# A decoder layer on one core: the attention's steps in another order on four engines, written out batch by batch

## Chip, core and metric

One core of one Trainium2 chip. The metric is the device time of one execution in microseconds (us). TensorE is called PE in the profile, VectorE DVE, ScalarE ACT, GpSimd POOL, and SyncE's DMA queue SPq.

## What is computed

One decoder layer on 16 batches of 128 rows of 128 numbers (float32): self-attention with 16 heads of 8 columns and rotary positions, a correlation step against a context, and a feed-forward part with 8 experts of which each row takes 2. After each of the three the input is added and the rows are normalised. Cut to the part that the change touches:

```python
qkv = jnp.einsum('bsd,ed->bse', x, w_qkv)            # x: (16, 128, 128)
q, k, v = ...                                         # 16 heads of 8
q, k = _apply_rope(q, cos, sin), _apply_rope(k, cos, sin)
scores = jnp.einsum('bhsd,bhtd->bhst', q, k) * SCALE
attn = jax.nn.softmax(scores, axis=-1)
out = jnp.einsum('bhst,bhtd->bhsd', attn, v)
x = _layernorm(x + out @ w_out.T + b_out)             # then correlation, then experts
```

## The kernel before

Each engine has a program of its own, a list of steps written by hand. Steps wait on semaphores for what they read and for buffers to come free; an engine never starts a step before the one ahead of it in its list. So the lists alone set the order, and no scheduler does.

**The stages.** The attention goes over the batches n = 0 to 15, several in flight at once. Then come the correlation step (one spectrum over all batches) and the experts in four groups of four batches. Only the attention's lists and the few steps beside them are touched here.

**One batch of the attention**, with the step's name in the code and the line of its instruction:

- PE `qkv(n)` (L965, L966) projects the batch; ACT `keep_qkv` (L706) copies the result from PSUM.
- The rotation is `rope_products` (L432, L438) and `rope_sum` (L444), on DVE for n = 0 and 1, on POOL from then on. Queries and keys are cut into three bf16 pieces, so that bf16 matmuls keep float32's precision: ACT `first_piece` (L719), POOL or DVE `remainder` (L450), ACT `second_piece` (L723) and `second_copy` (L727), POOL or DVE `third_piece` (L456). All land in `stack`, of which there are two.
- The keys are turned by PE `k_transposes` (L1003) and copied by ACT `kT_copy` (L732). The queries of batches 0 to 2 are turned by PE and copied by DVE; from batch 3 on SPq does it with a transposing DMA, `q_transpose` (L341).
- PE `scores(n, u)` (L981), u = 0 and 1 for the two halves of the heads, is reduced to row maxima by DVE `maxima` (L1383). `pieces_of_maxima` (L463, L465) makes two bf16 rows of them, PE `maxima_transpose` (L1028) turns these, ACT `mT_copy` (L745) copies them, and SPq `spread_maxima` (L348, two DMAs) spreads them into the query tile.
- PE `scoresT(n, u)` (L997) makes the same scores transposed, less the maxima; ACT `softmax_exp` (L737) takes the exponential into `early`; PE `weighted(n, u)` (L1042 and L1046) makes the weighted sums of `v_pad` and the denominators. `v_pad` is filled by POOL `pad_v` (L506).
- DVE `reciprocal` (L1394) and `divide` (L1399); PE `project` (L1059); DVE `residual_sum` (L1406), `statistics_of_rows` (L1419), `mean_and_variance` (L1424); POOL `inverse_deviation` (L493, L496); DVE `normal_rows` (L469).

`score_pair` and `scoreT_pair` each hold one half at a time: `scores(n, 1)` waits until `maxima(n, 0)` has read, and `scoresT(n, 1)` until `softmax_exp(n, 0)` has.

In the middle a loop `for k in range(8, 16)` gives every engine the same list for each k, with batch k at its first step and batch k-6 at its last ones. Ahead of it stands a list that fills the pipeline, behind it one that empties it.

**Beside the attention.** Four `w1_high_piece(i)` on ACT (L702) and four `w1_low_piece(i)` on POOL (L521) cut the experts' weight `w1` into two parts; piece i on POOL waits for piece i on ACT, and PE wants all four before its first expert matmul. `expand_v(g)` on POOL (L529) lays out the correlation's values. `residual(g)` on DVE (L1413) adds a bias to four batches of the input. `keep_clock(n)` on PE (L945, L951) is n matmuls into a free place, whose result nobody reads.

**Behind the attention**, untouched: ACT copies a spectrum (L751 to L753), makes two small parts (L842, L844) and takes the square root of the last batch's variance (`sd`, L846); DVE ends the last rows (L1549, L1552), PE ends the spectrum, DVE multiplies (L1561, L1565, L1566) and makes `lag` in two instructions (L1568, L1571), for which PE's next matmul (L1228) waits. POOL adds a bias to four groups of rows (`add_cross_bias`, L601): the first as soon as the last row is normal, the other three only when DVE has made `wsel` (L1588).

The two instructions that make `lag` read two operands from SBUF, as do L432 to L456, L465 and L1413:

```python
dve.scalar_tensor_tensor(lag[:, 0, :], sinm, reim[:, 1:2], part[:, 0, :], ALU.mult, ALU.add)
dve.scalar_tensor_tensor(lag[:, 1, :], sinm, reim[:, 0:1], part[:, 1, :], ALU.mult, ALU.subtract)
```

## Time and profile before

| | us |
|---|---|
| median of 3 runs | 232.91 |
| lowest and highest run | 232.44 and 234.08 |
| profiled execution, first to last instruction | 229.2 |
| PE busy | 215.3 (94%) |
| DVE busy | 181.3 (79%) |
| ACT busy | 142.5 (62%) |
| POOL busy | 111.6 (49%) |

The profile gives the profiled execution as its span, 229.2 us, which is 3.7 us under the median of the runs; those lie ahead of the first and behind the last instruction. The busy shares are averages over stages: in the attention all four engines are busy, in the experts PE and DVE alone. The end of a matmul is modelled, so that a PE that is never idle in a row may still have small gaps, which show between the starts.

### The profile page before, as it was taken

How to read it: one execution, taken by the hardware profiler on the slowest of the kernel's cores; microseconds unless marked ns; L12 is line 12 of the kernel's file. 1: busy time of each engine (PE TensorE's matmuls, PEld its weight loads, DVE VectorE, ACT ScalarE, POOL GpSimd, SP SyncE). 2: the span in 40 equal slices, each digit the busy share in tenths (PEclk: the TensorE clock that was granted, in tenths of full speed). 3: DMA queues.
4: the chain of work that ended last, by engine and by line, in shares of the span. 5: the costliest groups of instructions: out<-in, count | busy, mean ns of one | idle time of the engine just before them, and what ended most of it. 6: DMA issues, size and time to landing. Idle time of an engine off the chain costs nothing.

```text
span 229.2 us, 7210 instructions
## 1 busy us (share of the span) xinstructions
PE 215.3 (94%) x2724; PEld 184.4 (80%) x2724; DVE 181.3 (79%) x622; ACT 142.5 (62%) x248; POOL 111.6 (49%) x219
## 2 busy tenths in 40 slices
PE   8989899999999989999999999999999999999970
PEld 7766677778777667778887999789988999889970
DVE  0589998999899899776755779897798868875885
ACT  2488899999999995674489300991029610596112
POOL 5089889999889995513630400252002600040484
PEclk9999999999999999999999999999999999999996
DMA  5951534765569941000000000001000100001001
GB/s 149 286 124 34 106 61 51 171 133 119 138 125 156 156 90 19 14 3 1 3 0 0 3 0 1 0 3 46 4 0 0 46 3 1 0 4 46 1 16 34
DMA packets 32455, 12.32 MB, mean 54 GB/s; under 512 B 19907, under 2 KB 32291, under 8 KB 32419
## 3 DMA queue, kind: packets, MB, share of 16 engines
q1 hardware_dynamic: 31554, 11.48, 24.5%
q8 instruction: 22, 0.36, 0.7%
q10 hardware_dynamic: 864, 0.36, 0.6%
q14 instruction: 15, 0.11, 0.2%
HBM read 6.33 MB, written 1.05 MB: 32 GB/s over the span
## 4 chain that ended last, share of the span: by engine, by line
PE 81%; DVE 6%; DMA 5%; ACT 3%; issue 2%; SPq 1%; DVEq 0%; ACTq 0%
PE bank L1326 13%; PE scoreT_pair L1326 12%; PE score_pair L1298 11%; PE scoreT_pair L1298 8%; PE bank L1042 6%; PE bank L1046 5%; DMA qT_all<-mT 5%; PE bank L965 4%; PE scoreT_pair L997 4%; PE bank L1003 3%; PE score_pair L981 3%; PE scoreT_pair L945 2%; PE bank L1059 2%; ACT early L737 2%; PE bank L940 1%
## 5 line engine op out<-in xcount | busy, mean ns | idle before, releaser
L1383 DVE TENSOR_REDUCE rowmax<-score_pair 128x8 f32<-128x1024 f32 x32 | 39.0, 1218 | 3.3 <-PE score_pair L981 2.0
L608 POOL TENSOR_TENSOR ve<-mv,table 128x4 f32<-128x4 f32 (+1 forms) x12 | 3.3, 277 | 78.1 <-DVE mv L1743 60.2
L737 ACT ACTIVATE early<-scoreT_pair 128x1024 f32<-128x1024 f32 x32 | 32.9, 1027 | 6.0 <-PE scoreT_pair L997 5.9
L1326 PE MATMUL bank<-w,early 128*128 128x128 f32 x256 | 30.1, 276 | 0.0
L1326 PE MATMUL scoreT_pair<-w,early 128*128 128x128 f32 x256 | 29.9, 275 | 0.0
L1326 PEld LDWEIGHTS bank<-w,early 128*128 128x128 f32 x256 | 29.5, 192 | 0.3
L1326 PEld LDWEIGHTS scoreT_pair<-w,early 128*128 128x128 f32 x256 | 29.2, 192 | 0.0
L1298 PE MATMUL score_pair<-x2T_part,w_part 128*128 128x512 f32 x108 | 28.4, 397 | 0.0
L880 ACT ACTIVATE early<-score_pair,b 128x512 f32<-128x512 f32 x38 | 26.0, 691 | 3.2 <-PE score_pair L1298 2.6
L1042 PE MATMUL bank<-early,v_pad 128*32 128x128 f32 x512 | 26.5, 279 | 0.4 <-DVE attnT L1399 0.3
L1046 PE MATMUL bank<-early,head_ones 128*32 128x128 f32 x512 | 25.8, 273 | 0.0
L1298 PEld LDWEIGHTS score_pair<-x2T_part,w_part 128*128 128x128 f32 x108 | 19.6, 188 | 4.9 <-ACT early L880 1.4
L1298 PE MATMUL scoreT_pair<-x2T_part,w_part 128*128 128x512 f32 x78 | 19.9, 391 | 0.0
L1394 DVE RECIPROCAL rden<-bank 128x128 f32<-128x128 f32 x16 | 15.3, 956 | 4.2 <-PE bank L1046 4.1
L880 ACT ACTIVATE early<-scoreT_pair,b 128x512 f32<-128x512 f32 x26 | 17.6, 690 | 0.0
L1298 PEld LDWEIGHTS scoreT_pair<-x2T_part,w_part 128*128 128x128 f32 x78 | 14.6, 188 | 3.0
L732 ACT ACTIVATE kT_all<-bank 128x1024 bf16<-128x1024 bf16 x16 | 16.3, 1020 | 0.2 <-PE bank L1003 0.2
L1042 PEld LDWEIGHTS bank<-early,v_pad 128*32 128x32 f32 x512 | 12.7, 109 | 4.5 <-ACT early L737 1.4
L1046 PEld LDWEIGHTS bank<-early,head_ones 128*32 128x32 f32 x512 | 15.4, 110 | 0.0
L1731 DVE SCALAR_TENSOR_TENSOR x_ext<-bank,gate,x_ext 128x128 f32<-128x128 f32 x32 | 11.1, 346 | 4.7 <-PE bank L1326 4.7
L997 PE MATMUL scoreT_pair<-qT_all,kT_all 64*128 64x128 bf16 x256 | 12.7, 218 | 1.8 <-ACT early L737 0.7
L1731 DVE SCALAR_TENSOR_TENSOR x_ext<-scoreT_pair,gate,x_ext 128x128 f32<-128x128 f32 x32 | 11.1, 346 | 4.0 <-PE scoreT_pair L1326 3.7
(229 smaller groups left out, 474.0 us busy)
## 6 DMA issues: line engine op xcount, KB each, us to landing
w<-in_w SPq DMA_DIRECT2D x8, 256.0 KB, 3.8
x_ext<-in_x SPq DMA_DIRECT2D x4, 256.0 KB, 5.4
qT_all<-mT SPq DMA_DIRECT2D x32, 32.0 KB, 2.3
early<-in_xT SPq DMA_DIRECT2D x3, 256.0 KB, 4.5
early<-in_ctxT SPq DMA_DIRECT2D x3, 256.0 KB, 5.1
out<-qkv_all SPq DMA_DIRECT2D x3, 256.0 KB, 2.3
table<-in_tables SPq DMA_DIRECT2D x1, 321.0 KB
qT_all<-stack SPq DMA_TRANSPOSE x13, 3.4
```

The source lines that it names most:

```text
L732: act.activation(kT[n % DEEP][:, :, :], turned_slots, ACT.Copy).then_inc(s["k_T"], 1)
L737: act.activation(prob[n % 2][:, 2 * u:2 * u + 2, :, :], scoreT_pair[:, :].rearrange("p (i j s) -> p i j s", i=2, j=QUAD), ACT.Exp, scale=S ...
L880: act.activation(hT[:, c, :], hidden_bank(g, c)[:, :], ACT.Relu, bias=b1[:, c:c + 1])\
L965: pe.matmul(qkv_bank[:, 0:3 * D + XC], xT[:, n, :], wqkv[:, :], start=True, stop=True)
L997: mm = pe.matmul(scoreT_pair[:, (QUAD * side + j) * S:(QUAD * side + j + 1) * S], kT[n % DEEP][rows, 2 * j + u, :], qT[n % DEEP][rows, 2 * ...
L1042: pe.matmul(sum_bank(n)[WIDE * j:WIDE * (j + 1), 0:S], v_pad[n % 2][:, j, i, :], prob[n % 2][:, i, j, :], start=(i == 0), stop=(i == QUAD ...
L1046: mm = pe.matmul(sum_bank(n)[WIDE * j:WIDE * (j + 1), S:2 * S], head_ones[:, i * WIDE:(i + 1) * WIDE], prob[n % 2][:, i, j, :], start=Fals ...
L1298: mm = pe.matmul(hidden_bank(g, c)[:, :], w1_part[:, w, c * P:(c + 1) * P], x2T_part[:, x, :], start=(k == 0), stop=(k == 2))
L1326: mm = pe.matmul(expert_bank[k % 4][:, e4 * D:(e4 + 1) * D], hT[:, f, n * P:(n + 1) * P], w2[:, f, :], start=(c == 0), stop=(c == CH - 1))
L1383: dve.tensor_reduce(rowmax[:, H // 2 * u:H // 2 * (u + 1)], score_pair[:, :].rearrange("p (r t) -> p r t", t=S), AX_X, ALU.max).then_inc(s ...
L1394: dve.reciprocal(rden[:, :], sum_bank(n)[:, S:2 * S]).then_inc(s["rden_ready"], 1)
L1731: dve.scalar_tensor_tensor(total, product, weight, total, ALU.mult, ALU.add).then_inc(s["summed"], 1)
```

## The change

Only calls are moved. The loop over k on each of the four engines is replaced by its 8 rounds written out, each with an order of its own, and some steps ahead of and behind it move too. The steps themselves, their waits, their buffers and SPq's list are as before. Cut to what the text speaks of:

```diff
 # GpSimd, from batch 15's pieces on
-            pad_v(12)
-            w1_low_piece(0)
-            w1_low_piece(1)
-            w1_low_piece(2)
-            pad_v(13)
-            w1_low_piece(3)
-            pad_v(14)
-            inverse_deviation(8)
+            pad_v(12)
+            inverse_deviation(7)
+            w1_low_piece(0)
+            inverse_deviation(8)
+            pad_v(13)
...
+            inverse_deviation(12)
+            expand_v(1)
+            w1_low_piece(1)
             inverse_deviation(13)
             inverse_deviation(14)
+            w1_low_piece(2)
+            expand_v(2)
+            expand_v(3)
+            w1_low_piece(3)
 # ScalarE
             softmax_exp(11, 1)
-            w1_high_piece(0)
-            w1_high_piece(1)
-            w1_high_piece(2)
-            w1_high_piece(3)
             mT_copy(13)
             softmax_exp(12, 0)
             kT_copy(15)
             softmax_exp(12, 1)
+            w1_high_piece(0)
...
             softmax_exp(15, 1)
+            w1_high_piece(1)
+            w1_high_piece(2)
+            w1_high_piece(3)
 # TensorE, the fill
             qkv(0)
             keep_clock(3)
+            keep_clock(3)
             qkv(1)
-            keep_clock(3)
             turn_projection()
...
+            scores(2, 0)
             scoresT(0, 0)
-            scores(2, 0)
...
+            scores(3, 0)
             k_transposes(4)
             maxima_transpose(2)
             scoresT(1, 0)
-            scores(3, 0)
             qkv(7)
 # TensorE, the middle: round k = 9 of the eight
-                scoresT(k - 6, 0)
-                scores(k - 4, 0)
-                qkv(k)
-                project(k - 7)
-                scoresT(k - 6, 1)
-                scores(k - 4, 1)
-                weighted(k - 6, 0)
-                weighted(k - 6, 1)
-                k_transposes(k - 2)
-                maxima_transpose(k - 4)
+            scores(5, 0)
+            scoresT(3, 0)
+            maxima_transpose(4)
+            qkv(9)
+            k_transposes(6)
+            project(2)
+            scoresT(3, 1)
+            scores(5, 1)
+            weighted(3, 0)
+            weighted(3, 1)
 # VectorE, the fill
             third_piece(dve, 0)
-            residual(0)
             remainder(dve, 1)
             qT_copy(0)
-            keep_turned()
+            residual(0)
```

On TensorE, at the start of round k = 9 (`bank4` takes `qkv`, `bank5` the turned keys, `bank7` the turned maxima and the projection). Before, from the last two steps of round 8 on:

```order
L1003 MATMUL bank5<-ident16,stack0 128x128 x8
L1028 MATMUL bank7<-ident16,mstack 128x128
L997 MATMUL scoreT_pair<-qT_all,kT_all 128x128 x8
L981 MATMUL score_pair<-kT_all,qT_all 128x128 x8
L965 MATMUL bank4<-wqkv,early 128x392
L966 MATMUL bank4<-xwq,early 128x8
L1059 MATMUL bank7<-wo,attnT 128x136
L997 MATMUL scoreT_pair<-qT_all,kT_all 128x128 x8
```

The changed kernel at the same place (its lines stand 104 higher: L1085 is `scores`, L1101 `scoresT`, L1107 the keys' transposes, L1132 the maxima's):

```order
L1085 MATMUL score_pair<-kT_all,qT_all 128x128 x8
L1101 MATMUL scoreT_pair<-qT_all,kT_all 128x128 x8
L1132 MATMUL bank7<-ident16,mstack 128x128
L1069 MATMUL bank4<-wqkv,early 128x392
L1070 MATMUL bank4<-xwq,early 128x8
L1107 MATMUL bank5<-ident16,stack0 128x128 x8
L1163 MATMUL bank7<-wo,attnT 128x136
L1101 MATMUL scoreT_pair<-qT_all,kT_all 128x128 x8
```

The same eight pieces of work stand between the last `weighted` and the second `scoresT`: `scores` has gone to the front, the transposes behind it.

On ScalarE, from batch 15's keys on. Before (L702 is `w1_high_piece`):

```order
L732 ACTIVATE kT_all<-bank 128x1024
L737 ACTIVATE early<-scoreT_pair 128x1024
L702 ACTIVATE w_part<-w 128x512 x4
L745 ACTIVATE mT<-bank 128x128
L737 ACTIVATE early<-scoreT_pair 128x1024
L732 ACTIVATE kT_all<-bank 128x1024
```

The changed kernel, from its last `kT_copy` (L780) on (L785 is `softmax_exp`, L750 `w1_high_piece`, L793 `mT_copy`, L807 loads a function table):

```order
L780 ACTIVATE kT_all<-bank 128x1024
L785 ACTIVATE early<-scoreT_pair 128x1024
L750 ACTIVATE w_part<-w 128x512
L793 ACTIVATE mT<-bank 128x128
L785 ACTIVATE early<-scoreT_pair 128x1024 x2
L793 ACTIVATE mT<-bank 128x128
L785 ACTIVATE early<-scoreT_pair 128x1024 x4
L750 ACTIVATE w_part<-w 128x512 x3
L807 ACT_TABLE_LOAD
```

One of the four cuts of `w1` has moved back by four steps, the other three to behind the last exponential.

On GpSimd, around the end of the attention. Before:

```order
L493 TENSOR_TENSOR ve<-mv,table 128x1
L496 TENSOR_TENSOR rs<-ve,table 128x1
L601 TENSOR_TENSOR x_all<-x_all,bias 128x4x128
L635 TENSOR_TENSOR gate_w_part<-gate_w,gate_w_part 128x8
L601 TENSOR_TENSOR x_all<-x_all,bias 128x4x128 x3
```

The changed kernel (L649 is `add_cross_bias`):

```order
L529 COPY early<-x_ext 128x512
L521 TENSOR_TENSOR w_part<-w,w_part 128x512
L493 TENSOR_TENSOR ve<-mv,table 128x1
L496 TENSOR_TENSOR rs<-ve,table 128x1
L493 TENSOR_TENSOR ve<-mv,table 128x1
L496 TENSOR_TENSOR rs<-ve,table 128x1
L521 TENSOR_TENSOR w_part<-w,w_part 128x512
L529 COPY early<-x_ext 128x512 x2
L521 TENSOR_TENSOR w_part<-w,w_part 128x512
L649 TENSOR_TENSOR x_all<-x_all,bias 128x4x128
L683 TENSOR_TENSOR gate_w_part<-gate_w,gate_w_part 128x8
```

Three cuts of `w1` and three layouts of the values now stand around and behind the last two `inverse_deviation`, ahead of the first bias addition.

## Rows read from the trace of the kernel before

**Rows 1.** Busy time by stretch: us, then each engine's, PE's clock, DMA share, GB/s

```profile
0.00:33.20 33.20, 29.75 (x388) 23.82 (x390) 23.19 (x49) 22.63 (x40) 22.19 (x49) 1.00 0.53 124
33.20:73.20 40.00, 40.00 (x889) 31.44 (x888) 36.61 (x80) 38.14 (x65) 36.52 (x81) 1.00 0.63 130
73.20:98.90 25.70, 23.83 (x582) 17.86 (x580) 22.41 (x50) 21.02 (x31) 18.36 (x37) 1.00 0.49 69
98.90:107.90 9.00, 8.26 (x72) 7.51 (x69) 6.98 (x31) 4.51 (x14) 2.17 (x4) 1.00 0.00 1
```

**Rows 2.** Timeline of PE and its loads, one round: start, us, engine, line, what

```profile
55.06 0.40 PE L997 MATMUL scoreT_pair<-qT_all,kT_all 64*128 64x128 bf16 x8
...
56.57 0.43 PE L1042 MATMUL bank<-early,v_pad 128*32 128x128 f32 x8
...
57.59 0.62 PE L1003 MATMUL bank<-ident,stack 128*128 128x128 bf16 x8
```

**Rows 3.** Waits from 33 to 73 us: total, times, longest

```profile
ACT early L737 <- PE scoreT_pair L997: 1.9, 8, 0.2
...
PEld bank L1042 <- ACT early L737: 0.9, 6, 0.2
```

**Rows 4.** Timeline of SPq, then DMA issues at 44.2 and 59.2: KB, us to landing

```profile
58.75 1.24 SPq L348 DMA_DIRECT2D qT_all<-mT  x2
...
qT_all<-mT SPq DMA_DIRECT2D x2, 32.0 KB, 3.0
...
qT_all<-mT SPq DMA_DIRECT2D x2, 32.0 KB, 2.6
```

**Rows 5.** Timeline of the fill, ACT, DVE and PE

```profile
11.84 0.83 ACT L719 ACTIVATE stack<-qk 128x768 bf16<-128x768 f32 x1
...
12.34 0.88 DVE L1413 TENSOR_TENSOR x_ext<-x_ext,bias 128x512 f32<-128x512 f32 x1
...
22.72 0.40 PE L997 MATMUL scoreT_pair<-qT_all,kT_all 64*128 64x128 bf16 x8 [0.32 <-DMA qT_all<-mT]
...
28.40 0.39 PE L981 MATMUL score_pair<-kT_all,qT_all 48*128 48x128 bf16 x8
...
30.03 0.40 PE L997 MATMUL scoreT_pair<-qT_all,kT_all 64*128 64x128 bf16 x8
```

**Rows 6.** Timeline of ACT, batches 12 and 13

```profile
81.48 2.20 ACT L702 ACTIVATE w_part<-w 128x512 fp32r<-128x512 f32 x4
83.56 0.29 ACT L745 ACTIVATE mT<-bank 128x128 bf16<-128x128 bf16 x1
```

**Rows 7.** Timeline behind the last exponential, ACT, DVE and POOL

```profile
102.01 0.30 ACT L846 ACTIVATE sd<-mv,table 128x1 f32<-128x1 f32 x1 [0.78 <-DVE mv L1424]
...
100.72 0.18 DVE L1424 BATCH_NORM_AGGREGATE mv<-st 128x2 f32<-128x6 f32 x1
...
104.69 0.34 DVE L1568 SCALAR_TENSOR_TENSOR lag<-table,reim,part 65x128 f32<-65x128 f32 x1
...
100.98 0.19 POOL L493 TENSOR_TENSOR ve<-mv,table 128x1 f32<-128x1 f32 x1 [3.62 <-DVE mv L1424]
101.25 0.55 POOL L496 TENSOR_TENSOR rs<-ve,table 128x1 f32<-128x1 f32 x1
```

**Rows 8.** Timeline of POOL and DVE where both read SBUF, and where one does

```profile
78.59 1.73 POOL L529 COPY early<-x_ext 128x512 f32<-128x512 f32 x3
...
82.21 3.73 POOL L521 TENSOR_TENSOR w_part<-w,w_part 128x512 fp32r<-128x512 f32 x3 [0.47 <-ACT w_part L702]
...
81.55 0.23 DVE L463 CAST mstack<-rowmax 128x16 bf16<-128x16 f32 x1
...
85.39 0.59 DVE L463 CAST mstack<-rowmax 128x16 bf16<-128x16 f32 x1
...
9.90 0.42 DVE L450 TENSOR_TENSOR rest<-qk,stack 128x256 f32<-128x256 f32 x1
...
13.15 0.61 DVE L450 TENSOR_TENSOR rest<-qk,stack 128x256 f32<-128x256 f32 x1
```

More of the change, by code:

```diff
@@ L1482, in _ @@
             divide(1)
[L1483 to L1493 removed]
+            maxima(4, 0)
+            residual_sum(1)
+            maxima(4, 1)
@@ new lines, in _ @@
+            pieces_of_maxima(dve, 4)
+            reciprocal(2)
+            divide(2)
+            maxima(5, 0)
+            normal_rows(dve, 0)
+            maxima(5, 1)
+            pieces_of_maxima(dve, 5)
+            residual_sum(2)
+            statistics_of_rows(1)
+            reciprocal(3)
+            divide(3)
+            maxima(6, 0)
+            residual_sum(3)
+            statistics_of_rows(2)
+            maxima(6, 1)
+            mean_and_variance(1)
+            pieces_of_maxima(dve, 6)
@@ new lines, in _ @@
+            statistics_of_rows(3)
+            mean_and_variance(2)
+            reciprocal(4)
+            divide(4)
+            maxima(7, 0)
+            maxima(7, 1)
+            normal_rows(dve, 1)
+            residual_sum(4)
+            pieces_of_maxima(dve, 7)
+            reciprocal(5)
+            mean_and_variance(3)
+            statistics_of_rows(4)
+            divide(5)
+            maxima(8, 0)
+            maxima(8, 1)
+            mean_and_variance(4)
+            residual_sum(5)
@@ L1540, in _ @@
             statistics_of_rows(14)
+            normal_rows(dve, 13)
             mean_and_variance(14)
```

360 lines of the change are left out of this document (276 added, 84 removed).

## The prediction

> **What bounds the kernel now.** Read the busy time by stretch first [rows 1]. From 33.2 to 73.2 us the eight rounds of the middle run, 40.0 / 8 = 5.0 us each, and PE has no idle time; ACT is busy 38.1 of the 40, DVE 36.6, POOL 36.5. PE's idle time lies in the fill (33.2 - 29.75 = 3.45, of which about 1.0 is the start) and in the emptying (25.7 - 23.83 = 1.87). Everything behind 107.9 us is as before, so the change is worth what it does to the end of the attention and to the 9 us behind it.
>
> Next one round on PE [rows 2]. I count from T, the start of what follows the second `weighted` (57.59). From T to the second `scoresT` of the next round stand the keys' transposes, the maxima's transpose, `scoresT`, `scores`, `qkv` and `project`: 55.06 - (57.59 - 5.0) = 2.47 us with no gap. From that `scoresT` to the second `weighted` are 1.51 us (56.57 - 55.06), in which PE waits for the exponential: 0.9 us in six rounds [rows 3], 0.15 each. From there to T are 1.02. The three make 5.0. So the loop is closed on PE, but for 0.15 a round in which ACT holds it; ACT in turn waits 0.23 a round for PE [rows 3], and is no bound of its own.
>
> **The change, part by part.**
>
> The middle, 8 rounds. The same matmuls stand between T and the second `scoresT`: 2.47 us again. The exponential still hangs on that `scoresT`, so the 1.51 and the 1.02 stay. What could be won is only the 0.15 where PE waits, and only if work moves from ahead of `scoresT(n, 1)` to behind it; that happens in one round (k = 15, where `project` does). Against it stand a few more changes between float32 and bf16 matmuls, and one round (k = 11) in which DVE gets `normal_rows`, `residual_sum` and `statistics_of_rows` between its maxima and the next `divide`, so that `maxima(8, 0)`, on which `scores(8, 1)` waits, is some 0.2 late. I take 0.0. The ends: 0.9 to the good (every wait of rows 3 gone), and the wait of the rival below to the bad.
>
> The fill. Three things:
> - `residual(0)`, 0.88 us on DVE [rows 5], stood ahead of the second batch's `remainder`. That `remainder`, at 13.15 [rows 8], had its input from 11.84 + 0.83 = 12.67 on [rows 5]; the second `keep_clock(3)` ahead of `qkv(1)` makes that input about 0.2 later, by delaying batch 1, so `remainder` can start near 12.9, 0.25 earlier. `residual(0)` takes some of this back ahead of `third_piece(1)`: I carry 0.15 on, through `scores(0, 0)`, the maxima and the first spread, to `scoresT(0, 0)` at 22.72 [rows 5].
> - `scores(2, 0)` no longer stands behind that DMA wait, which makes DVE's `maxima(2, 0)` some 0.8 earlier. `scoresT(1, 0)` doesn't gain by it: it waits for the next spread, issued from an `mT_copy` that still stands behind `softmax_exp(0, 0)`. So it is again 0.15 earlier.
> - `scores(3, 0)` stood between `scoresT(1, 0)` and `scoresT(1, 1)`: it took the first 0.32 of the 1.63 us from 28.40 to 30.03 [rows 5]. It now stands ahead, in PE's wait.
>
> Together 0.15 + 0.3 = 0.45 us earlier into the middle. Ends: 0 (DVE's chain `reciprocal(0)`, `maxima(3, 0)` takes the end, since two `residual` now stand ahead of it) and 1.0.
>
> The emptying. The four cuts of `w1` on ACT, from 81.48 to 83.56 [rows 6], stood ahead of `mT_copy(13)`. They leave; of their 2.08 us about 0.4 to 0.7 reach the exponentials of batch 12. Later `project(11)` and `project(12)` move ahead of a `scoresT`, or behind, and a spread of maxima (batch 14) is the last to come in both. Following the waits to the last `weighted` I find 0.65 us ahead of before, 0.2 more than at the end of the fill. Ends: 0 and 0.7.
>
> Behind the attention, ACT. Three of the cuts, 3 x 2.08 / 4 = 1.56 us, now stand between the last exponential and `sd`. Before, ACT waited 0.78 for DVE there [rows 7] and 0.52 ahead of the spectrum, 1.30 together. Since the last exponential itself comes about 0.9 earlier and the row that `sd` waits for only 0.65, the new finish of ACT's list falls within 0.1 of that row. Cost 0.05; ends 0 and 0.4.
>
> Behind the attention, POOL. POOL's `inverse_deviation(14)` starts with the batch's variance, 100.98 against DVE's 100.72 [rows 7], and lasts until 101.80. The changed list goes on without a wait: a cut of 1.25 us (3.73 / 3), two layouts of 0.58 (1.73 / 3), a cut of 1.25 [rows 8]. In the times of before that is 101.9 to 103.15, then 104.3, then 105.55; then comes the first bias addition. DVE makes `lag` at 104.69 [rows 7] and right behind it, inside the last cut, and both instructions read two operands from SBUF. In the trace before POOL is idle there. What such an overlap costs is shown in two places [rows 8]. DVE's cast of the maxima takes 0.23 us at 81.55 and 0.59 at 85.39, under the third cut of the row at 82.21, which ends near 85.9; it ends only with it. DVE's `remainder` takes 0.42 us at 9.90 with POOL idle, 0.61 at 13.15 with POOL busy. So DVE waits for the rest of POOL's instruction: 105.55 - 104.69 = 0.86. I take 0.8. Ends: 0 (this form of instruction doesn't wait) and 1.9 (POOL's next 1.25 us instruction gets in between the two).
>
> The Trainium skill says this in "SBUF — State Buffer", section "Who interferes with whom": a VectorE instruction with two SBUF inputs contends with a GpSimd instruction that reads SBUF, and whichever was issued second blocks until the first is done. By that rule, the trace agrees for `remainder` and the cast (0.42 and 0.61 us; 0.23 and 0.59), and no row shows `scalar_tensor_tensor` in that position. With it the sum is the one below; without it, 0.8 less.
>
> The sum: 0.0 - 0.45 - 0.2 + 0.05 + 0.8 = +0.2 us. The span goes from 229.2 to 229.4 and the time from 232.91 to 233.1.
>
> **Rivals.**
> - *`lag` isn't held up.* Then only the lead is left: -0.6, 232.3 us. For it: no row has this form beside POOL, and POOL may be out of step by half a microsecond. Against: POOL is busy without a break for some 4 us around the place.
> - *It is held up twice.* 1.9 in place of 0.8: 234.2 us. For it: POOL's next instruction waits already when the first `lag` ends.
> - *PE's idle time is filled.* The orders differ in every round, and I followed only the waits that bind before. If half of what PE idles in fill and emptying behind the start (2.45 + 1.87) and half the 0.9 of the middle go, that is 2.6 us: 230.3. Against: the fill hangs on two DMA chains that stay.
> - *Slower: the spread of the maxima lands late.* The first `scoresT` of a round comes 0.4 to 0.6 us sooner after T than before, at T or T + 0.23, while its maxima are spread as late as ever: `mT_copy` ends near T + 1.15 (58.75, rows 4), the second DMA is issued 0.62 later and lands 2.6 to 3.0 us after that [rows 4], at T + 4.4 to 4.8, against 5.0. It decides from a landing of 3.3 us on. If the transposed queries, whose `second_copy` in some rounds is later, shift the queue so that landings take 3.6, each round waits 0.3: 8 x 0.3 = 2.4, 235.5 us. Against it: in the rounds seen the landings leave 0.2 to 0.6.
>
> **How the numbers follow.** A change of 1% is about what a measurement of this kernel can tell from none. The forecast (233.1, give or take 0.6) gets 0.38, `lag` free 0.25, held twice 0.13, idle time filled 0.11, late spread 0.13. Under 230.6 lies most of the fourth case, over 235.2 most of the last: faster by over 1% 0.10, within 1% 0.78, slower by over 1% 0.12. The range goes from 231.2 (the ends of fill, emptying and half the middle together) to 235.0, short of the late spread.
>
> **What would show it.** The eight rounds at 5.0 us each with PE never idle. The first `scoresT(1, 0)` near 28.0 and the second `weighted(1, 1)` done near 32.1. No wait of PE for `qT_all` from 33 to 72 us. The last exponential near 96 us and `sd` near 101.4 without a long wait. The first `lag` instruction over 1 us long, with POOL in a cut. The forecast is wrong if a round isn't 5.0 us, by eight times the difference, or if POOL has its last cut behind it before `lag`.

## The result, and the profile after

The changed kernel takes 235.53 us (median of 5 runs, 235.28 to 240.67) where the kernel before takes 232.91 (5 runs, 231.36 to 234.39): ratio 1.015, 95% interval 1.010 to 1.020. A second trial of both gave 236.06 against 231.9, 1.016 (1.013 to 1.019). The forecast was 233.1 and its range ended at 235.0. The 240.67 is of an execution in a second, slower state and doesn't count in the ratio.

The profiled execution took 237.35 us, its span is 235.5 (before 229.2). In every execution whose time and span are both on record the time is 1.75 to 1.95 us over the span. So, as an estimate, the profiled execution of before took some 231.1 us: of the 3.7 us between its span and the median of the runs only half lie ahead of the first and behind the last instruction, and the rest is that this execution was a quick one. The same three stretches as in [rows 1], cut at the same events in the changed kernel:

```profile
35.40:77.40 42.00, 39.56 (x885) 31.26 (x883) 39.48 (x80) 39.20 (x66) 37.24 (x83) 1.00 0.66 118
77.40:102.60 25.20, 23.61 (x578) 18.17 (x580) 20.83 (x50) 19.14 (x28) 12.35 (x30) 1.00 0.49 78
102.60:114.30 11.70, 8.73 (x81) 7.61 (x72) 10.42 (x33) 6.05 (x16) 7.30 (x11) 1.00 0.01 2
```

The fill ends 2.2 us later than before (35.4 against 33.2), the middle takes 42.0 instead of 40.0, the emptying 25.2 instead of 25.7, and what follows 11.7 instead of 9.0. In the middle PE, without idle time before, idles 2.4 us, and DVE is busy 39.5 us with the same 80 instructions that took 36.6.

I set the two traces side by side by events that both have: the first exponential of batches 0, 2 and 10, the last exponential, and the second `x2T_part` of DVE (L1646, L1879 after), from which to the end of the span both need 114.7 us. All are starts.

| us | before | after | difference |
|---|---|---|---|
| start to the first exponential | 23.16 | 25.08 | +1.92 |
| from there to batch 2's | 10.45 | 10.70 | +0.25 |
| batch 2's to batch 10's (the middle) | 40.04 | 42.05 | +2.01 |
| batch 10's to the last exponential | 23.19 | 22.78 | -0.41 |
| from there to the second `x2T_part` | 17.69 | 20.28 | +2.59 |
| from there to the end | 114.67 | 114.66 | 0 |

These are +6.3 us, while the timed runs differ by 2.6 to 4.2. The first line is the reason: it is a matter of the single run, as the next paragraph shows.

**The first line.** The twelve matmuls of the two `keep_clock(3)` in the changed kernel's trace, then in those of three experiments told of below: *tail_undone* and *mt10_early*, which have the changed fill, and *middle_only*, which has the fill of before (its last four are of `keep_clock(2)`). One `keep_clock(3)` shows as six instructions.

```profile
7.03 2.91 PE L1049 MATMUL scoreT_pair<-mean_w 128*128 128x128 f32 x12
```
```profile
5.77 1.58 PE L1049 MATMUL scoreT_pair<-mean_w 128*128 128x128 f32 x12
```
```profile
6.73 1.58 PE L1049 MATMUL scoreT_pair<-mean_w 128*128 128x128 f32 x12
```
```profile
7.03 1.63 PE L1049 MATMUL scoreT_pair<-mean_w 128*128 128x128 f32 x6
...
10.04 1.16 PE L1049 MATMUL scoreT_pair<-mean_w 128*128 128x128 f32 x6
...
11.26 0.61 PE L1049 MATMUL scoreT_pair<-mean_w 128*128 128x128 f32 x4
```

The same instructions in the same list take 0.24 us each in one execution and 0.13 in another. The matmuls of the first 3.7 us have the slow pace in every trace; the step to the faster one comes between 3.8 and 6.7 us in fourteen of the twenty traces and past 8 us in six, in either order of the list. The granted clock reads 1.00 in all of these windows, which is the level of 2.4 GHz, so the record doesn't show it. The 1.9 us are chance. With the step at 3.9 us the changed fill reaches its first exponential at 22.62 and batch 2's at 32.96 (*tail_undone*); with the step near 6 us, as in the trace of before, at 22.94 and 33.62 (*lows_late*), where before needed 23.16 and 33.61. So with the pace of before the changed fill is 0.2 ahead at the first exponential and level at batch 2's. With the step between 4 and 5.1 us in both it is 0.3 to 0.5 ahead at batch 2's (33.20 in *act_regular* and *pool_regular*, 33.54 to 33.72 in *mt10_late*, *end_only* and *keep_ahead*, which have the fill of before).

The fill has a second matter of chance, and only in its changed order. *mt10_early* has the pace of before (its `keep_clock` starts at 6.73 in both), and its first exponential still comes at 24.54. Here are DVE's second `remainder` (L450) and POOL's `rope_products` (L438) in *lows_late* and in *mt10_early*:

```profile
12.56 0.42 DVE L450 TENSOR_TENSOR rest<-qk,stack 128x256 f32<-128x256 f32 x1 [0.54 <-ACT stack L768]
12.57 1.03 POOL L438 TENSOR_TENSOR rot<-qkv_all,table 128x128 f32<-128x128 f32 x2
```
```profile
12.69 0.68 DVE L450 TENSOR_TENSOR rest<-qk,stack 128x256 f32<-128x256 f32 x1 [0.54 <-ACT stack L767]
12.69 0.93 POOL L438 TENSOR_TENSOR rot<-qkv_all,table 128x128 f32<-128x128 f32 x2
```

The two start within 0.01 us of each other, and one holds the other: DVE takes 0.42 and POOL's first 0.68, or DVE 0.68 and POOL's first 0.39. Of the ten traces with the changed fill on all engines seven went the first way and reached the first exponential 10.4 to 10.7 us behind this `remainder`; three went the second (*mt10_early*, *fill_and_round*, *keep_behind*) and needed 11.9, 13.2 and 13.5. With the fill of before it is 10.0 in all nine traces.

**The middle.** DVE's two cuts of the maxima, from 33.6 to 73.6 us before and from 35.8 to 77.8 after (groups by line: count | busy, mean ns | idle ahead):

```profile
L465 DVE TENSOR_TENSOR mstack<-rowmax,mstack 128x16 bf16<-128x16 f32 x8 | 1.6, 196 | 0.3
L463 DVE CAST mstack<-rowmax 128x16 bf16<-128x16 f32 x8 | 1.4, 178 | 0.0
```
```profile
L463 DVE CAST mstack<-rowmax 128x16 bf16<-128x16 f32 x8 | 3.1, 382 | 0.1
L465 DVE TENSOR_TENSOR mstack<-rowmax,mstack 128x16 bf16<-128x16 f32 x8 | 2.6, 328 | 0.3
```

2.7 of the 2.9 us by which DVE's busy time grew are in these sixteen instructions. The timeline of the changed kernel shows how, in the round that became 5.47 us long:

```profile
43.95 0.68 POOL L456 TENSOR_TENSOR stack<-rest,stack 128x256 bf16<-128x256 f32 x1
43.95 0.72 DVE L463 CAST mstack<-rowmax 128x16 bf16<-128x16 f32 x1
...
44.58 0.73 POOL L432 TENSOR_TENSOR rot<-qkv_all,table 128x256 f32<-128x256 f32 x1
44.70 0.66 DVE L465 TENSOR_TENSOR mstack<-rowmax,mstack 128x16 bf16<-128x16 f32 x1
45.27 0.29 DVE L1579 TENSOR_TENSOR y<-bank,x_ext 128x136 f32<-128x136 f32 x1
45.70 0.22 PE L1132 MATMUL bank<-ident,mstack 128*128 128x128 bf16 x1 [0.59 <-DVE y L1579]
45.95 0.28 ACT L793 ACTIVATE mT<-bank 128x128 bf16<-128x128 bf16 x1 [0.59 <-PE bank L1132]
```

Each cut ends with POOL's instruction beside it (44.67 and 44.63, 45.36 and 45.31), and the chain behind it, transpose, copy, spread, is late by that. The transpose itself waits last for `residual_sum` (L1579), which DVE's changed list has behind the cuts of this round and no longer ahead of them: it empties the bank that the transpose writes. Of the sixteen cuts eight are held like this (0.28 to 0.72). In the eight rounds of before the cuts stand beside POOL's `inverse_deviation`, whose two instructions are on 128x1, and none is held:

```profile
57.01 0.19 POOL L493 TENSOR_TENSOR ve<-mv,table 128x1 f32<-128x1 f32 x1
57.06 0.18 DVE L463 CAST mstack<-rowmax 128x16 bf16<-128x16 f32 x1
57.27 0.20 DVE L465 TENSOR_TENSOR mstack<-rowmax,mstack 128x16 bf16<-128x16 f32 x1
57.28 0.59 POOL L496 TENSOR_TENSOR rs<-ve,table 128x1 f32<-128x1 f32 x1
```

The longest round of after is the last, 6.04 us:

```profile
71.79 1.02 ACT L785 ACTIVATE early<-scoreT_pair 128x1024 f32<-128x1024 f32 x1
72.86 0.42 ACT L775 ACTIVATE stack<-rest 128x256 bf16<-128x256 f32 x1
73.18 0.26 ACT L793 ACTIVATE mT<-bank 128x128 bf16<-128x128 bf16 x1
...
73.47 1.27 SPq L348 DMA_DIRECT2D qT_all<-mT  x2
...
77.39 0.40 PE L1101 MATMUL scoreT_pair<-qT_all,kT_all 64*128 64x128 bf16 x8 [0.63 <-DMA qT_all<-mT]
...
77.83 1.02 ACT L785 ACTIVATE early<-scoreT_pair 128x1024 f32<-128x1024 f32 x1 [0.76 <-PE scoreT_pair L1101]
```

`mT_copy(10)` is the only one of the middle that stands behind the batch's exponential and a copy. PE had the transpose ready at 71.80 (71.57 + 0.23); SyncE issues the spread by the copy at 73.18, and 4.2 us later it lets PE go.

**Behind the attention.** DVE, POOL and ACT of the changed kernel, to hold against [rows 7]:

```profile
102.23 1.28 POOL L521 TENSOR_TENSOR w_part<-w,w_part 128x512 fp32r<-128x512 f32 x1 [1.56 <-ACT w_part L750]
102.59 1.00 DVE L469 TENSOR_SCALAR x_all<-y,mv,rs 128x136 f32<-128x136 f32 x1
...
106.22 1.27 POOL L521 TENSOR_TENSOR w_part<-w,w_part 128x512 fp32r<-128x512 f32 x1
106.28 1.28 DVE L469 TENSOR_SCALAR x_all<-y,mv,rs 128x136 f32<-128x136 f32 x1
106.39 0.30 ACT L950 ACTIVATE sd<-mv,table 128x1 f32<-128x1 f32 x1 [0.47 <-DVE mv L1597]
...
107.68 0.99 DVE L1785 TENSOR_SCALAR x_all<-y,mv,rs 128x8 f32<-128x8 f32 x2
...
109.78 1.26 POOL L649 TENSOR_TENSOR x_all<-x_all,bias 128x512 f32<-128x512 f32 x1
109.83 1.30 DVE L1799 TENSOR_SCALAR part<-table,reim 65x128 f32<-65x128 f32 x1
...
111.05 0.34 DVE L1801 SCALAR_TENSOR_TENSOR lag<-table,reim,part 65x128 f32<-65x128 f32 x1
```

`lag` is 0.34 long, as before, and stands beside POOL only for 0.15 us, beside a product on 128x8 (L683, 0.20 long, at 111.01). It is the `tensor_scalar` instructions ahead of it that end with POOL's: `normal_rows` 1.00 and 1.28 instead of 0.34, `part` 1.30 instead of 0.28. What holds `part` is the first bias addition (L649), which the moved pieces have pushed to there; before, it ran at 103.01, ahead of `part`.

### The profile page after: what moved, and what is told of

It reads as the page before. It is cut to its first block, busy times and chain, and to the rows that moved or that the text cites. A ratio compares the mean times of both kernels' runs of the same rounds, so it can differ in the third digit from the quotient of the medians.

```text
span 235.5 us, 7210 instructions
## 1 busy us (share of the span) xinstructions
PE 216.9 (92%) x2724; PEld 186.2 (79%) x2724; DVE 186.6 (79%) x622; ACT 143.9 (61%) x248; POOL 111.4 (47%) x219
## 3 DMA queue, kind: packets, MB, share of 16 engines
q1 hardware_dynamic: 31554, 11.48, 25.2%
## 4 chain that ended last, share of the span: by engine, by line
PE 60%; POOL 11%; DVE 9%; issue 5%; DMA 3%; ACT 2%; SPq 1%; DVEq 0%; POOLq 0%; ACTq 0%
PE bank L1499 12%; PE scoreT_pair L1499 12%; PE score_pair L1471 11%; PE scoreT_pair L1471 8%; PE bank L1146 3%; DMA qT_all<-mT 3%; PE bank L1150 2%; POOL rot L438 2%; PE scoreT_pair L1101 2%; POOL rest L450 2%; POOL qk L444 2%; POOL stack L456 2%; PE score_pair L1085 1%; PE bank L1163 1%; ACT early L785 1%
## 5 line engine op out<-in xcount | busy, mean ns | idle before, releaser
L785 ACT ACTIVATE early<-scoreT_pair 128x1024 f32<-128x1024 f32 x32 | 32.8, 1025 | 5.2 <-PE scoreT_pair L1101 4.5
L780 ACT ACTIVATE kT_all<-bank 128x1024 bf16<-128x1024 bf16 x16 | 16.3, 1018 | 0.3 <-PE bank L1107 0.3
L432 POOL TENSOR_TENSOR rot<-qkv_all,table 128x256 f32<-128x256 f32 x14 | 10.3, 736 | 10.9 <-DVE qk L444 10.2
L1101 PE MATMUL scoreT_pair<-qT_all,kT_all 64*128 64x128 bf16 x256 | 12.7, 218 | 2.6 <-DMA qT_all<-mT 1.3
```

The costliest lines, as they stand in the source:

```text
L432: eng.tensor_tensor(rot[:, 0, :].rearrange("p (h d) -> p h d", d=HD), qkv_all[:, n, 0:2 * D].rearrange("p (h d) -> p h d", d=HD), cosines, ...
L780: act.activation(kT[n % DEEP][:, :, :], turned_slots, ACT.Copy).then_inc(s["k_T"], 1)
L785: act.activation(prob[n % 2][:, 2 * u:2 * u + 2, :, :], scoreT_pair[:, :].rearrange("p (i j s) -> p i j s", i=2, j=QUAD), ACT.Exp, scale=S ...
L1101: mm = pe.matmul(scoreT_pair[:, (QUAD * side + j) * S:(QUAD * side + j + 1) * S], kT[n % DEEP][rows, 2 * j + u, :], qT[n % DEEP][rows, 2 * ...
```

## The experiments

Four questions: what the start costs, what is lost behind the attention, what the middle loses, and whether a gain is left. "Stretch" is from the first exponential of batch 2 to that of batch 10 (before 40.04, after 42.05); "tail" from the last exponential to the last `lag` (before 8.11, after 10.70).

**The changed kernel once more (*again*), no edit.**

> The changed kernel, word for word, a second time. In its first profile the twelve keep_clock matmuls ahead of qkv(1) took 2.69 us (0.224 each), where the kernel before took 0.125 each, and the fill came 1.9 us late; its execution was 1.9 us longer than its other runs. Theory A (the slow first matmuls are chance, and the order costs about 2.6 us elsewhere): the matmuls take about 0.125 each in this profile, the first exponential comes near 23.2 us, and the median stays at 1.010 to 1.020 of before. Theory B (the second keep_clock(3) itself brings the slow matmuls on): 0.22 each again, first exponential near 25.1 us.

1.016 (1.013 to 1.019); the trace again has the slow pace up to past 10 us, stretch 42.4, tail 10.71. That left both theories of the start open; *tail_undone*, with the same list in the fill, decided for chance, and *middle_only* showed the slow pace with the list of before (first exponential 25.02).

**The pieces of the first layer back (*tail_undone*).** In the changed kernel, on ScalarE and GpSimd:

```
 ACT  softmax_exp(11, 1)
+     w1_high_piece(0) ... w1_high_piece(3)
 POOL ...
+     w1_low_piece(0) ... (3), expand_v(1) ... (3)
      inverse_deviation(8) ... inverse_deviation(14)
-     w1_low_piece(2), expand_v(2), expand_v(3), w1_low_piece(3)
```

> The changed kernel with the cuts of w1 and the layouts of the values back where they were: all four w1_high_piece behind softmax_exp(11, 1), the w1_low_piece and expand_v ahead of pad_v(15). Theory A (DVE's chain behind the last exponential is held up by GpSimd's long instructions, 2.5 us of the loss between the last weighted and lag): from the last weighted to lag 6.4 us as before, and the time falls by 2.0 to 2.5 us against the changed kernel, to 0.998 to 1.006 of before. Theory B (that stretch is long because ScalarE's cuts delay the square root): then it should gain 0.5 at most more than GpSimd's moved work alone gives. Rival: the loss sits in the middle and this gives under 1 us.

1.013 (1.008 to 1.017), where theory A had 0.998 to 1.006. The tail is 8.18, and DVE's instructions have their old lengths:

```profile
105.48 0.32 DVE L469 TENSOR_SCALAR x_all<-y,mv,rs 128x136 f32<-128x136 f32 x1
106.13 0.54 DVE L1788 TENSOR_SCALAR x_all<-y,mv,rs 128x8 f32<-128x8 f32 x2
...
108.05 0.28 DVE L1802 TENSOR_SCALAR part<-table,reim 65x128 f32<-65x128 f32 x1
```

So the placement of these pieces makes the whole 2.5 us of the tail. The time fell by less, 1.016 to 1.013 with intervals that overlap: the four cuts in a row ahead of `mT_copy(13)` are back too, and from batch 10's exponential to the last it is 25.2 us instead of 22.8.

**The last pieces later still (*lows_late*).**

```
 POOL inverse_deviation(14)
-     w1_low_piece(2), expand_v(2), expand_v(3), w1_low_piece(3)
      add_cross_bias(0), gate_w_rest()
+     wait for circ_ready; expand_v(2), expand_v(3), w1_low_piece(2), w1_low_piece(3)
```

> The changed kernel, where GpSimd's w1_low_piece(2) and (3) and expand_v(2) and (3) wait for wsel and so run behind lag; ScalarE's cuts stay at the end. If the loss behind the attention is VectorE waiting for GpSimd's instructions, all of them behind inverse_deviation(14) are gone and 1.5 to 2.0 us of the 2.5 come back (the first cut, which holds one normal_rows up, stays). If it is ScalarE's cuts ahead of the square root, nothing comes back.

Half right: the tail is 8.68, 2.0 us back, but the time 1.018 (1.014 to 1.022), nothing gained. Up to the second `x2T_part` it is 20.37 again: the bias additions, pushed back, now hold the normalized rows of the next step (L1877), which take 0.34 each in the changed kernel and here 0.58, 1.30, 1.11 and 0.34:

```profile
114.36 3.70 POOL L645 TENSOR_TENSOR x_all<-x_all,bias 128x512 f32<-128x512 f32 x3
...
115.13 1.80 DVE L1877 TENSOR_SCALAR x<-y,mv,rs 128x128 f32<-128x128 f32 x2
...
117.04 1.37 DVE L1877 TENSOR_SCALAR x<-y,mv,rs 128x128 f32<-128x128 f32 x2
```

**Only the placement of the pieces, in the kernel before (*cuts_late*)**: ScalarE's first cut behind `softmax_exp(12, 1)` and three behind the last exponential, GpSimd's pieces around and behind the last two `inverse_deviation`, all else as before.

> Before, with only the pieces of the first layer and the expansions of v placed as in the changed order: ScalarE's first cut behind softmax_exp(12, 1) and three behind the last exponential, GpSimd's remainders of them and expand_v(1) to (3) around and behind inverse_deviation(13) and (14). Theory A (this placement alone makes the loss behind the attention, by holding VectorE's tensor_scalar operations): last exponential to last lag 10.5 to 10.8 us instead of 8.1; the exponentials of 12 to 15 come up to 0.8 earlier, without four cuts in a row ahead of mT_copy(13); ratio 1.007 to 1.012. Theory B (it needs the changed order of the inverse deviations and VectorE's late rows as well): 8.1 to 9.2 and 0.997 to 1.004.

1.009 (1.006 to 1.013); tail 10.22, two normalizations of 0.9 and two of 0.84 in it:

```profile
104.38 1.77 DVE L469 TENSOR_SCALAR x_all<-y,mv,rs 128x136 f32<-128x136 f32 x2
106.27 1.68 DVE L1788 TENSOR_SCALAR x_all<-y,mv,rs 128x8 f32<-128x8 f32 x2
```

The placement alone makes 2.1 of the 2.6 us. The exponentials of batches 12 to 15 did not come earlier: batch 10's to the last took 23.6.

**The changed order from the last rounds on (*end_only*), and only in the middle (*middle_only*).** Both are the kernel before, with each engine's list switched to the changed one at `weighted(9, 1)`, `mT_copy(11)`, `divide(9)`, `pad_v(11)`, or from `weighted(1, 1)`, `mT_copy(3)`, `divide(1)`, `pad_v(3)` up to there.

> Before up to weighted(9, 1), mT_copy(11), divide(9) and pad_v(11), and from there on the changed order: the last rounds, the emptying, the first layer's pieces and inverse_deviation. Theory A (GpSimd's late pieces stand in DVE's way behind the attention, and that costs 2.6 us whatever stood ahead): last exponential to the last lag 10.6 to 10.8 us against 8.1, the emptying within 0.5 of before, 1.009 to 1.013 of the kernel before. Theory B (they fall there only since the whole middle came 2 us later to the end; handed over on time they are done before the deviations are wanted): last exponential to the last lag 8.1 to 9.0, ratio 0.998 to 1.004.

1.009 (1.006 to 1.013), stretch 40.34, emptying 23.3, tail 10.70: theory A, with the middle handed over on time. One round of the untouched part, around 48 us, took 5.45: PE waits there for a spread of maxima, as it does in *keep_ahead* (5.28) and *mt10_late* (5.75), and not in the trace of before.

> Before, with the changed order on all four engines only in the rounds of the middle: from where weighted(1, 1), mT_copy(3), divide(1) and pad_v(3) end to where weighted(9, 1), mT_copy(11), divide(9) and pad_v(11) do; the fill, the emptying and what stands behind the attention are those of before. Theory A (the rounds of the middle cost about 2.0 us themselves: from the first exponential of batch 2 to that of batch 10 the changed kernel took 42.05 us and before 40.04): 1.0065 to 1.0100 of the kernel before (233.5 to 234.3), the same stretch 41.5 to 42.2 us. Theory B (the middle is late only because the changed fill hands its chains over in another phase, POOL's and the spread's above all): 0.998 to 1.003, the stretch 40.0 to 40.6.

1.019 (1.015 to 1.023). The time is over theory A's 1.010. The stretch is 42.18, as theory A has it; the rest of the loss is where the changed middle meets the old end, with 4.84 us between the two exponentials of batch 10 (2.44 before) and an emptying of 25.99 (23.20). Neither the changed fill nor the changed end is needed for the 2.0 us.

**One copy in the middle, out and in.** *mt10_early* is the changed kernel and *mt10_late* the kernel before, with on ScalarE

```
 mt10_early                      mt10_late
+mT_copy(10)                    -mT_copy(10)
 softmax_exp(9, 0)               softmax_exp(9, 0)
 second_copy(13)                 second_piece(13), second_copy(13)
-mT_copy(10)                    +mT_copy(10)
```

> The changed kernel with one step moved on ScalarE: mT_copy(10) ahead of softmax_exp(9, 0), where every other one of these copies stands, and not behind second_copy(13). Theory A (this place made the round from 71.79 to 77.83 us, 6.04 long: the copy at 73.18, the spread at 73.47, and scoresT(10, 0) at 77.39 waited for it): the round takes 4.9 to 5.1, the kernel 0.9 to 1.1 us less than the changed one (235.0 to 235.2, ratio 1.011 to 1.013). Theory B (DVE and GpSimd hold the end of that round anyway, and PE only waits for whichever is last): the round stays 5.6 to 6.0 and the time within 0.3 us of the changed one's 236.06.

1.012 (1.008 to 1.016), no difference from the changed kernel that the intervals show. The trace:

```profile
71.09 0.28 ACT L793 ACTIVATE mT<-bank 128x128 bf16<-128x128 bf16 x1
71.27 1.02 ACT L785 ACTIVATE early<-scoreT_pair 128x1024 f32<-128x1024 f32 x1
...
71.82 1.26 SPq L348 DMA_DIRECT2D qT_all<-mT  x2
...
76.20 0.40 PE L1101 MATMUL scoreT_pair<-qT_all,kT_all 64*128 64x128 bf16 x8
```

The wait for the spread is gone and the round is 5.37 instead of 6.04, but the exponential ahead of it came 0.2 later, so the stretch is 41.61: 0.45 back, not 1.0, and the emptying took it again (23.3 against 22.8; the changed kernel's second trace has 23.2 as well).

> Before, with one step moved on ScalarE: mT_copy(10) behind softmax_exp(9, 0), second_piece(13) and second_copy(13), as the changed order has it but with no other difference. Theory A (this place costs the round some 1 us, since the spread of these maxima is issued by it and scoresT(10, 0) stands behind the spread's landing): the step from the first exponential of batch 9 to that of batch 10 6.0 to 6.9 us instead of 5.0, the kernel 0.9 to 1.9 us over before (1.004 to 1.008). Theory B (before has slack there that the changed order had lost): 5.0 to 5.4, ratio under 1.002.

1.011 (1.002 to 1.020). The round is 6.16 instead of 5.0 and the emptying 24.15 instead of 23.19. Put into a kernel that had no other fault the step costs its 1.2 us and, in this trace, 0.95 more behind it. The stretch is 41.83: a further 0.75 is the round of 5.75 around 48 us, ahead of the step and not its doing.

**TensorE's rounds alone (*pe_round*).** The kernel before with its eight rounds on PE in the order of the changed kernel's first:

```
-k_transposes(k-3), maxima_transpose(k-5), scoresT(k-6, 0), scores(k-4, 0), qkv(k), project(k-7)
+scores(k-4, 0), scoresT(k-6, 0), maxima_transpose(k-5), k_transposes(k-3), qkv(k), project(k-7)
```

> The kernel before, with one thing of the change: in all eight rounds TensorE has the order of the changed kernel's first round (scores, scoresT, maxima_transpose, k_transposes, qkv, project, scoresT, scores, weighted twice); the other engines' lists are those of before. In the changed kernel's profile the rounds k = 8 and 9 took 4.86 and 4.83 us against 5.0, and from the first scores to the second scoresT 2.33 against 2.48. Theory A (fewer changes between float32 and bf16 matmuls; TensorE closes the round): all eight rounds at 4.85, 1.2 us in all, 0.993 to 0.996 of before. Rival (ScalarE and VectorE have no room for it, or the spread of the maxima lands late): rounds of 5.0 or more and no gain.

0.998 (0.996 to 1.001), stretch 39.36. Rounds of 4.9, but the first came 0.5 late, and what the rest won ended at batch 14's spread, for which PE waits 0.52 at 91.31 us. This order of TensorE's costs nothing; the orders of its other rounds were not run alone.

**The lists of the middle in halves (*pe_act_mid*, *dve_pool_mid*)**: as *middle_only*, but only two engines changed.

> Before, with the changed order in the rounds of the middle on TensorE and ScalarE alone (the late mT_copy(10) among it), VectorE and GpSimd as before. Theory A (VectorE and GpSimd make the 1.1 us that the late copy leaves, since the work of the same 80 VectorE operations grew from 36.6 to 39.5 us by holding): from the first exponential of batch 2 to that of batch 10 40.5 to 41.2 us, the 5.4 to 6 us round of the copy alone long, L463 at 0.18. Theory B (the order in which ScalarE hands over its pieces moves GpSimd's, and by that VectorE's maxima cuts are held): 41.6 to 42.4, L463 over 0.30.

1.002 (0.996 to 1.008), stretch 41.70 with a last round of 5.92: as theory B has it, but L463 took only 0.27 and L465 0.20. What makes these rounds long is the spread of the maxima: PE waits for it in five of them, 0.16 to 0.74 us, 2.0 in all.

> Before, with the changed order in the rounds of the middle on VectorE and GpSimd alone, TensorE and ScalarE as before. Theory A (these two make the 1.1 us): from the first exponential of batch 2 to that of batch 10 41.0 to 41.5 us, L463 over 0.30 on average. Theory B (ScalarE's order makes it, and GpSimd's fits ScalarE's): under 40.6, or, if GpSimd's changed list doesn't fit ScalarE's of before, above 42 with long waits of GpSimd for ScalarE.

1.031 (1.025 to 1.036), stretch 43.61, with the waits of GpSimd for ScalarE and back that the last clause named:

```profile
POOL rot L432 <- ACT qkv_all L754: 6.0, 4, 1.9
...
ACT stack L771 <- POOL rest L450: 3.0, 3, 1.1
```

The halves cost 1.7 and 3.6, together 2.0. So what one engine's list costs depends on the other three, and no fixed share of the loss belongs to one of them.

**One engine's list put back (*pool_regular*, *act_regular*, *dve_before*)** in the changed kernel: GpSimd's in rounds 9 to 14, ScalarE's in the eight rounds, VectorE's throughout.

> The changed kernel with GpSimd's steps of the rounds 9 to 14 in the even order of before (small columns, remainder, products, pad, sum, third piece, one batch after another), each inverse_deviation left a round late as the changed order has it; the other engines as changed. Theory A (the middle's loss comes from GpSimd's two-input operations, which now run in the moments in which VectorE cuts the maxima: L463 and L465 took 0.41 and 0.35 on average against 0.18 and 0.20): those go back to under 0.25 each in the stretch from 46 to 72 us and the first exponential of batch 10 comes 0.7 to 1.1 us earlier after that of batch 2 (41.0 to 41.4 instead of 42.05); the time 1.010 to 1.013 of before. Theory B (VectorE's own order and the late mT_copy(10) make all of it): 41.8 to 42.2 and the time as the changed kernel's.

1.022 (1.017 to 1.027): theory A fell. L465 went back to 196 ns, L463 only to 325, and the stretch grew to 42.54, since PE now waits four times for the spread of the maxima.

> The changed kernel with ScalarE's list of before in the eight rounds of the middle. Theory A (ScalarE's order alone makes the loss of the middle): 40.0 to 40.8 us from batch 2's first exponential to batch 10's. Theory B (the four lists of the changed order are fitted to each other and cost more apart, as GpSimd's did): over 42.0.

1.027 (1.019 to 1.035), stretch 43.97: theory B. The cuts of the maxima took 0.27 on average here, less than in the changed kernel, in a stretch 1.9 us longer.

> The changed kernel with VectorE's list of before, the other three engines as changed. Theory A (in the middle it is VectorE's order that makes rounds of 5.2 to 5.5 us: a sum, a reciprocal or the pieces of the maxima one place later than the transpose or the copy that waits for them): the stretch from batch 2's first exponential to batch 10's falls from 42.05 to 40.4 to 41.0 us and the time to 1.008 to 1.011 of before. Theory B (GpSimd's longer chain of rotation, remainder and third piece makes them, and VectorE is only held by it): 41.7 to 42.2 us, the time within 0.3 us of the changed kernel's or above it.

1.063 (1.058 to 1.068), the worst of all: VectorE's `normal_rows` waits once for 6.6 us for an `inverse_deviation` that GpSimd's list has a round later.

**The other suspect on ScalarE (*keep_ahead*, *keep_behind*)**: `keep_qkv(k)` ahead of `first_piece(k-1)` in four rounds of before, and behind it in the rounds k = 10 to 15 of the changed kernel, with `mT_copy(10)` early.

```
+keep_qkv(10)
 first_piece(9)
-keep_qkv(10)
```

> Before, with ScalarE's keep_qkv(8), (10), (12) and (14) each one place earlier, ahead of first_piece(7), (9), (11) and (13). The piece comes 0.5 us later, which GpSimd's remainder and SyncE's q_transpose wait for. Theory A (this makes rounds of the changed order long): the four rounds behind them are 5.2 to 5.5 us and the stretch from batch 2's first exponential to batch 10's 40.8 to 42.0; ratio 1.003 to 1.008. Theory B (the piece had the time, since the remainder of this batch is cut late anyway): 40.0 to 40.4, ratio under 1.002.

0.999 (0.995 to 1.004), stretch 40.32: it costs nothing.

> The changed kernel with mT_copy(10) ahead of softmax_exp(9, 0) and every keep_qkv(k) behind first_piece(k-1), the rest of ScalarE's list as changed. Theory A (the copies ahead of the pieces make the 1.1 us that the late mT_copy(10) leaves): from batch 2's first exponential to batch 10's 40.3 to 41.0 us, where mt10_early took 41.61 and the changed kernel 42.05; ratio 1.007 to 1.010. Theory B (the cuts of the maxima held by GpSimd make it): 41.4 to 41.9, ratio as mt10_early's 1.012.

1.028 (1.020 to 1.035), where *mt10_early* had 1.012 and both theories expected no more: taking it out made the kernel slower. The suspicion is void both ways.

**Is a gain left (*fill_only*, *fill_and_round*)?** The kernel before with the changed fill, and with that and PE's rounds of *pe_round*.

> Before, with the changed order only in the fill, up to weighted(1, 1) on TensorE, mT_copy(3) on ScalarE, divide(1) on VectorE and pad_v(3) on GpSimd. Theory A (the fill itself gains 0.4 to 0.5 us, and the first exponential of the changed kernel at 25.1 instead of 23.2 was the clock of TensorE at the start, which comes early or late in either order): ratio 0.996 to 1.000, and the first exponential at 22.6 to 23.0 where the clock is up early, 24.5 to 25.1 where it is not. Theory B (the second keep_clock(3) ahead of qkv(1) and the changed fill cost 1.9): ratio 1.005 to 1.009 whatever the clock does.

1.002 (0.999 to 1.005). The trace fell on a late change of pace, first exponential at 24.95, as theory A allows; from there to batch 2's it takes 10.74 where before takes 10.45. A gain of the fill is not to be found in the time.

> Before, with the changed fill on all four engines and the changed order of TensorE's eight rounds, and the rest as before: the parts that neither trace holds anything against. Theory A (their gains of 0.4 and 0.3 us stand side by side): 0.995 to 0.999 of before. Theory B (a round's gain is taken back by the spread of batch 14's maxima, as when it ran alone, and the fill's by the rounds, which a fixed wait paces): 0.999 to 1.001.

0.998 (0.994 to 1.002), no difference. In its trace the pace is up before 5.1 us and the first exponential still comes at 25.37, with `remainder` held (0.68): *fill_only*'s theory A, which had 22.6 to 23.0 for an early pace, missed this. No version beat the kernel before beyond its interval.

## Why the prediction was wrong

It forecast +0.2 us. In runs of like pace the changed kernel has 0.0 to -0.5 in the fill; by the table it has +2.0 in the middle, -0.4 in the emptying and +2.6 behind the attention, +3.7 to +4.2 together; the timed runs have 1.5 to 1.6% of 232, 3.4 to 3.7. Two terms failed: the middle, put at 0.0, and GpSimd behind the attention, put at 0.8. Both of the signs that the forecast itself named for being wrong came true: rounds of 4.88 to 6.04 us, and POOL through with its last cut (109.82) before `lag` (111.05).

- **The fill, -0.45: not confirmed.** In *tail_undone* `scoresT(1, 0)` starts at 27.79 (28.0 forecast, 28.16 before) and the second `weighted(1, 1)` is done at 32.03 (32.1 forecast, 32.63 before), but there the faster pace came some 2 us before that of the trace of before. In *lows_late*, with the pace of before, it is 28.44 and 32.70: nothing gained. *fill_only* found nothing in the time. That the second `keep_clock(3)` makes batch 1's first piece 0.2 later isn't seen: 11.84 before, 11.83 in *mt10_early*. The forecast had neither matter of chance of the fill, the pace (1.9 us from run to run) and the held `remainder` (with it the first exponential comes 1.1 to 3.2 later).
- **The middle, 0.0: the step that failed first.** It was argued from PE alone: "the same matmuls stand between T and the second `scoresT`". On PE this is right as far as it was tested (*pe_round*). But in [rows 1] DVE, ACT and POOL are busy 36 to 38 of 40 us, and a list in another order moves what stands beside what. The forecast priced one late DVE step, 0.2, and took it as 0; it did not follow `mT_copy(10)`, although it gave the time from `mT_copy` to landing that decides (rival four). Nor did it ask in which moments POOL's two-operand instructions run against DVE's cuts of the maxima, though [rows 8] had the price. What the runs showed in its place is +2.0 us (42.05 against 40.04, and 42.18 in *middle_only*), of which the late copy makes 0.5 to 1.2.
- **The late spread as a rival, 235.5 us at 0.13: its time came true, its place only in part.** It named eight rounds by 0.3. The trace has no wait for `qT_all` in most rounds, one of 0.35 near 55 us and one of 0.63 at 77.39, and that one comes from a late copy, not from a slow landing. With the changed lists on PE and ACT alone (*pe_act_mid*) the wait is there in five rounds.
- **The emptying, -0.2: within the scatter.** It is -0.41 in this trace and -0.04 in the changed kernel's second, and +0.1 with the middle of before (*end_only*).
- **ACT's three cuts ahead of `sd`, +0.05: right.** `sd` waits 0.47 for DVE, so ACT is not the last.
- **POOL holds `lag` up, +0.8 (0 to 1.9): the right engine and mechanism, the wrong instructions, and a third of the size.** The forecast looked for instructions with two SBUF operands and found `lag`, which starts at 111.05 only when POOL's bias addition has ended. Those held are `tensor_scalar`: five of them, 0.66 + 0.94 + 0.45 + 1.02 = 3.1 us longer, of which 2.6 reach the end. They had the same mark in the trace as the cast of [rows 8], one SBUF tensor in and one out, which the forecast itself had cited as held. The Trainium skill's rule in "SBUF — State Buffer", section "Who interferes with whom", was taken in its words on two SBUF inputs. The same section of the Trainium skill names `cast` and `tensor_scalar` among the forms that can contend with GpSimd, which are the held ones here; the forecast left that out, and put the cast, which reads one tensor, under the rule on two. The step that failed is this choice of what POOL holds: the term measured 2.6, and put back in their place the pieces cost nothing in the tail (*tail_undone*). The second half of the rule, that the instruction issued second blocks until the first is done, is what the rows show: L469 starts at 106.28, 0.06 behind POOL's, and both end near 107.5.

What stays open is most of the middle's 2.0 us. The late copy gave back 0.45 where it was taken out (*mt10_early*) and cost 1.2 where it was put in (*mt10_late*), so 0.8 to 1.6 have no shown cause. The cuts held by GpSimd are seen in the trace and not shown as its cause, since the one run that moved them (*pool_regular*) freed the second cut and lost more by other waits, and since *act_regular* and *pe_act_mid* have long stretches with fewer held cuts. The place of `residual_sum` behind the cuts was not run alone either.

## What to carry to other kernels

In a steady loop whose engines are all busy over nine tenths, a new order on the lists is not judged by the engine that never idles: ask for each engine which instruction of another stands beside it, and which copy lets a DMA go, and take those two, not the count of matmuls. A piece of background work moved behind the critical stretch is not free when it runs on GpSimd: it lengthens what VectorE does beside it, and moving it again moves the loss. Lists that were made together can't be mended one at a time; single steps added to the good version gave prices that can be read, steps taken out of the bad one mostly did not. And two instructions that start within 0.01 us of each other on engines that hold each other make a kernel's time a matter of chance: look at more than one trace of the same list.

## What the runs showed of the hardware

- VectorE's `tensor_scalar` on float32 in SBUF, 128 x 136, took 0.34 us alone and 1.00 to 1.28 beside a GpSimd `tensor_tensor` of 1.27, ending within 0.1 of it; so did 65 x 128 (0.28 and 1.30). The instructions that read PSUM were not held: the product of L1794 took 0.42 at 108.67 inside a GpSimd instruction from 108.56 to 109.83, and 0.42 before.
- Two-input instructions of VectorE and GpSimd held each other here, and a near tie can go either way: with starts 0.004 to 0.011 us apart DVE's L450 took 0.42 and POOL's L438 0.68 in seven traces, 0.68 and 0.39 in three. Beside GpSimd's `tensor_tensor` on 128x1 VectorE's cast and `tensor_tensor` on 128x16 were not held (0.18 and 0.20 beside 0.19 and 0.59, in all eight rounds of the kernel before).
- TensorE ran the matmuls of the start at half its later pace until some moment between 3.8 and 6.7 us or past 8, differently from execution to execution of one program (*again*, *lows_late* and *act_regular* have the same list there), with the granted clock at 1.00. A single profile of such a kernel can be 1.9 us off by this alone.
- One stretch of SyncE's queue differs from run to run as well: the issue of a transposing DMA took 1.27 us in the median of all traces and 1.5 to 2.5 in 49 of 260, in either order.
